# Last 512 tokens of the second shared experts as two groups of 256, two routed results summed per chunk, idle products in TensorE's first holes

## What is computed

```
x = x + layernorm(attention(layernorm(x)))        # 32 heads of 8, 8 key/value heads, rotary, causal
x = x + layernorm(ffn(layernorm(x)))

# ffn, per token xt:
scores = sigmoid(xt @ w_router.T)                 # 8 experts, top 2, weights normalised to sum 1
out  = sum over the 2 chosen experts of weight * (silu(xt @ wg.T) * (xt @ wu.T)) @ wd.T
out += sum over the 2 shared experts of (silu(xt @ sg.T) * (xt @ su.T)) @ sd.T      # inner width 640
```

## Time and profile before

| | us |
|---|---|
| three timed runs, median | 674.14 |
| timed runs, lowest and highest | 672.01, 674.25 |
| profiled execution | 669.11 |
| its span, first to last instruction | 667.4 |
| TensorE busy | 634.4 (95%) |
| VectorE busy | 531.4 (80%) |
| ScalarE busy | 417.1 (63%) |
| GpSimd busy | 327.6 (49%) |

### The profile page before, as it was taken

The page is one execution under the profiler, slowest core; times in us unless marked ns, Lnnn a source line. Parts: engine busy times, 40 slices in busy tenths (PEclk is TensorE's granted clock), DMA queues, the critical chain, the costliest instruction groups (busy, mean ns, idle before and its releaser), DMA issues.

```text
span 667.4 us, 15193 instructions
## 1 busy us (share of the span) xinstructions
PE 634.4 (95%) x5872; PEld 511.4 (77%) x5872; DVE 531.4 (80%) x1052; ACT 417.1 (63%) x782; POOL 327.6 (49%) x519
## 2 busy tenths in 40 slices
PE   8888899999999979999998999999999999999994
PEld 6634455555555547888888999999999999888883
DVE  5789999999988743479769888888988888468885
ACT  2526688888887875542247877877877787422230
POOL 3225657766666762100275464455454530178854
PEclk9958999999999999999999999999999999999998
DMA  3954543657350000000366786877776764032221
GB/s 90 174 125 66 116 82 66 124 104 155 90 107 13 18 11 17 16 1 1 119 225 222 264 273 224 262 242 267 229 256 240 253 224 145 20 92 91 84 64 47
DMA packets 79671, 87.10 MB, mean 131 GB/s; under 512 B 54352, under 2 KB 69072, under 8 KB 79600
## 3 DMA queue, kind: packets, MB, share of 16 engines
q0 software_dynamic: 11872, 54.53, 24.8%
q1 hardware_dynamic: 67456, 31.21, 20.2%
q10 hardware_dynamic: 272, 0.39, 0.2%
HBM read 63.83 MB, written 9.31 MB: 110 GB/s over the span
## 4 chain that ended last, share of the span: by engine, by line
PE 75%; DVE 10%; issue 4%; ACT 3%; SPq 2%; POOL 2%; DMA 1%; another core or an unknown queue 1%; POOLq 0%; DVEq 0%; ACTq 0%
PE PS L539 71%; DVE NM L1031 3%; DVE NM L1027 2%; PE PS L550 2%; PE PS L745 1%; ACT PF L886 1%; SPq L1540 1%; SPq L1546 1%; POOL PF L1449 1%; POOL RS L1392 1%; ACT WH L841 1%; DVE X L1296 1%; DVE RR L992 1%; DVE WL L1315 1%
## 5 line engine op out<-in xcount | busy, mean ns | idle before, releaser
L1236 DVE TENSOR_TENSOR HF<-SS,PS 128x256 f32<-128x256 f32 (+2 forms) x141 | 68.7, 487 | 72.3 <-ACT SS L932 34.3
L1315 DVE TENSOR_TENSOR WL<-RAW,WH 128x768 fp32r<-128x768 f32 x125 | 118.4, 958 | 7.7 <-ACT WH L841 7.3
L932 ACT ACTIVATE SS<-PS 128x256 f32<-128x256 f32 (+2 forms) x141 | 62.0, 439 | 87.6 <-PE PS L539 75.9
L1449 POOL TENSOR_SCALAR_AFFINE_SELECT PF<-PF 128x512 f32<-128x512 f32 x128 | 83.2, 673 | 58.4 <-ACT PF L886 58.4
L539 PE MATMUL PS<-WH,HH 128*128 128x256 f32 x355 | 103.2, 291 | 1.3 <-DVE ACC L1246 0.8
L841 ACT ACTIVATE HH<-HF 128x256 fp32r<-128x256 f32 (+1 forms) x120 | 58.0, 484 | 73.3 <-DVE HF L1236 63.0
L841 ACT ACTIVATE WH<-RAW 128x768 fp32r<-128x768 f32 x125 | 103.4, 841 | 0.0
L886 ACT ACTIVATE PF<-PS 128x1536 f32<-128x1536 f32 x64 | 92.8, 1450 | 16.8 <-PE PS L539 15.2
L539 PE MATMUL PS<-WL,HH 128*128 128x256 f32 x355 | 100.3, 282 | 0.0
L539 PE MATMUL PS<-WH,HL 128*128 128x256 f32 x355 | 100.2, 282 | 0.0
L539 PE MATMUL PS<-XGH,WH 128*128 128x256 f32 x320 | 90.4, 282 | 1.7 <-DVE WL L1315 1.0
(11 more groups left out here) (203 smaller groups left out, 1429.2 us busy)
## 6 DMA issues: line engine op xcount, KB each, us to landing
ys<-YO SPq DMA_DIRECT2D x16, 256.0 KB
RAW<-in_wsh SPq DMA_DIRECT2D x4, 768.0 KB, 4.9
XT<-in_xt SPq DMA_DIRECT2D x8, 256.0 KB, 3.7
X<-in_x SPq DMA_DIRECT2D x8, 256.0 KB, 3.7
xn<-YY SPq DMA_DIRECT2D x16, 128.0 KB, 1.7
out<-X SPq DMA_DIRECT2D x16, 128.0 KB
ys<-YO SPq DMA_DIRECT2D x7, 128.0 KB
RAW<-in_wsh SPq DMA_DIRECT2D x2, 384.0 KB, 5.3
```

The source lines that it names most:

```text
L932: eng.activation(ss, both(i, bank(b))[0], ACT.Silu).then_inc(free[b] if dense(i) else silu, 1)
L1236: eng.tensor_tensor(hf, ss, both(c, bank(b))[1], ALU.mult).then_inc(free[b], 1)
L1315: eng.tensor_tensor(WL[q % 2][:, c], RAW[raw_of(q)][:, c], WH[q % 2][:, c].bitcast(F32), ALU.subtract).then_inc(w_lo, 1)
L1449: eng.affine_select(out=o, in_=o, pattern=[[0, 4], [1, 128]], base=0, channel_multiplier=-1, compare_op=ALU.is_ge, fill=0.0).then_inc(zero ...
```

## The change

1. The last group of 512 tokens of the second shared experts (tiles 12 to 15) becomes two groups of 256 tokens. `HALF` is the first chunk of these (136), and there are 146 chunks in all. `up` makes products of 256 columns there, `down` two parts in place of four, the first of the two groups in bank 4, the second in bank 5. Tiles 12 and 13 are combined and finished within the chunks; only tiles 14 and 15 are left for `last`. From `HALF` on one tile a chunk goes to `o_stats` and `finish`, in place of two.
2. `mix` goes two tiles a chunk in chunks 125 to 129 (0 to 9), then one a chunk until `mix 15` in chunk 135. GpSimd's gathers move with it.
3. Idle products: 35 behind `f_qkv 3` (34 before), 13 behind `early 0` (14 before), and new ones: 5 behind `early 1`, 3 behind `early 2`, 2 behind `early 3`.
4. `FRONT0` is a quarter step earlier from `f_qkv` on; `FRONT1` has `f_third`, `f_fourth`, `q`, `k`, `k_twice` one or two quarter steps later. On SyncE the transposes of tiles 2 and 3 come as q 2, k 2, q 3, k 3 in place of k 2, q 2, k 3, (loads and `constants()`), q 3: the loads and constants go with `k 3` and so stand behind both transposes. `b_route` is a quarter step earlier and one leftover attention step moves from ahead of chunk 4 to ahead of chunk 3.

```diff
-CHUNKS += [(NK + 1, c % IC, 1) for c in range(DENSE)]
+HALF = len(CHUNKS) + DENSE - IC
+CHUNKS += [(NK + 1, c % IC, 1) for c in range(DENSE + IC)]
...
-WARM = {"mean": (0, 12), "f_qkv": (3, 34), "early": (0, 14), "late": (0, 6)}
+WARM = {("mean", 0): 12, ("f_qkv", 3): 35, ("early", 0): 13, ("late", 0): 6, ("early", 1): 5, ("early", 2): 3, ("early", 3): 2}
 JOIN = 64
-LAST4 = NT - 4
+FINAL = NT - 2
...
-FRONT0 = {"f_stats": -108, "f_dev": -111, "f_qkv": -87, "f_taken": -87, "f_rope": -83, "f_first": -81, "f_second": -80,
-          "f_third": -77, "q": -77, "k": -74, "k_first": -81, "k_third": -80, "f_fourth": -77, "k_twice": -73}
+FRONT0 = {"f_stats": -108, "f_dev": -111, "f_qkv": -88, "f_taken": -88, "f_rope": -84, "f_first": -82, "f_second": -81,
+          "f_third": -78, "q": -78, "k": -75, "k_first": -82, "k_third": -81, "f_fourth": -78, "k_twice": -74}
 FRONT1 = {"f_stats": -98, "f_dev": -95, "f_qkv": -77, "f_taken": -78, "f_rope": -78, "f_first": -78, "f_second": -71, "f_third":
-          -68, "q": -60, "k": -59, "k_first": -77, "k_third": -71, "f_fourth": -67, "k_twice": -66}
+          -67, "q": -58, "k": -57, "k_first": -77, "k_third": -71, "f_fourth": -65, "k_twice": -64}
...
-        "b_norm2": 66, "b_turn2": 70, "b_high": 69, "b_low": 68, "b_route": 75, "b_kept": 73}
+        "b_norm2": 66, "b_turn2": 70, "b_high": 69, "b_low": 68, "b_route": 74, "b_kept": 73}
...
-TAILS = (3, 2, 1, 2, 2, 3, 1, 1, 3, 3, 1, 2, 1, 3)
+TAILS = (3, 2, 1, 3, 1, 3, 1, 1, 3, 3, 1, 2, 1, 3)
...
-        if LAST + 4 <= c < LAST + 2 + NT:
-            m = c - LAST - 2
-            out.extend(("mix", i) for i in ((2 * m - 4, 2 * m - 3) if m < 4 else (m,)))
+        if LAST + 4 <= c < HALF:
+            m = c - LAST - 4
+            out.extend(("mix", i) for i in ((2 * m, 2 * m + 1) if m < NT - 11 else (m + NT - 11,)))
         if c < NC + 1:
             out.extend(("finish", i) for i in done)
-            done = stats[:2]
-            stats = stats[2:]
+            n = 1 if c >= HALF else 2
+            done = stats[:n]
+            stats = stats[n:]
             out.extend(("o_stats", i) for i in done)
         elif c == NC + 1:
-            for t in range(4):
-                out.append(("last", LAST4 + t))
-            out.extend(("finish", LAST4 + t) for t in range(4))
+            for t in range(2):
+                out.append(("last", FINAL + t))
+            out.extend(("finish", FINAL + t) for t in range(2))
...
                     for m in range(2):
-                        o = bank(take(("up", c, m)))
+                        o = both(c, bank(take(("up", c, m))))[m]
...
-                parts = n if narrow(c) else 4 if dense(c) else 2
+                parts = wide_of(c) // 128
                 for k in range(parts):
-                    b = 4 + k // 2 if dense(c) else 4 + q % 2
+                    b = 4 + (c - HALF) // IC if c >= HALF else 4 + k // 2 if dense(c) else 4 + q % 2
```

More of the change, by code:

```diff
@@ L85, in wide_of, with tiles_of, group_of @@
 def wide_of(c):
-    return 128 * CHUNKS[c][2] if narrow(c) else 256 if DENSE <= c < LAST else 512
+    return 128 * CHUNKS[c][2] if narrow(c) else 256 if DENSE <= c < LAST or c >= HALF else 512
+def tiles_of(c):
+    if c >= HALF:
+        return range(NT - 4 + 2 * ((c - HALF) // IC), NT - 2 + 2 * ((c - HALF) // IC))
+    return range(4 * ((c if c < DENSE else c - LAST) // IC), 4 * ((c if c < DENSE else c - LAST) // IC) + 4)
+def group_of(i):
+    return LAST + IC * (i // 4) if i < FINAL else HALF + IC
 def ends(c):
@@ L286, in banks @@
         elif s[0] == "down" and CHUNKS[s[1]][1] == 0:
-            for b in (4 + sequence(s[1]) % 2,) if DENSE <= s[1] < LAST else (4, 5):
+            for b in (4 + sequence(s[1]) % 2,) if DENSE <= s[1] < LAST else (4 + (s[1] - HALF) // IC,) if s[1] >= HALF else (4, 5):
                 count[b] += 1
@@ L647, in up @@
                 if dense(c):
-                    tg = (c if c < DENSE else c - LAST) // IC
-                    for t in range(4):
-                        read(e, ("b_turn2", 4 * tg + t))
+                    n = wide_of(c)
+                    t0 = 128 * tiles_of(c)[0]
+                    for t in tiles_of(c):
+                        read(e, ("b_turn2", t))
                     for m in range(2):
-                        o = bank(take(("up", c, m)))
+                        o = both(c, bank(take(("up", c, m))))[m]
                         k6 = 0
@@ L748, in idle @@
             def idle(s):
-                i, n = WARM[s[0]]
-                for _ in range(n if s[1] == i else 0):
+                for _ in range(WARM.get(s, 0)):
                     mm(bank(7, 256, 384), mean[:, :], mean[:, :], True)
@@ L1238, in combine @@
             def combine(c):
-                tg = (c if c < DENSE else c - LAST) // IC
                 e.wait_ge(dn, c + 1)
-                for q in (2, 3, 0, 1) if c == DENSE - 1 else range(4):
-                    i = 4 * tg + q
+                tiles = tiles_of(c)
+                for i in (*tiles[2:], *tiles[:2]) if c == DENSE - 1 else tiles:
+                    q = i % 4
                     b, k = use["down", c - IC + 1, 4 + q // 2]
@@ L1343, in _ @@
                     q = i % 4
-                    b, k = use["down", LAST + IC * (i // 4), 4 + q // 2]
+                    b, k = use["down", group_of(i), 4 + q // 2]
                     e.wait_ge(free[b], k)
@@ L1349, in _ @@
                 elif what == "last":
-                    t = i - LAST4
-                    b = use["down", NC - IC, 4 + t // 2][0]
-                    if t % 2 == 0:
-                        e.wait_ge(dn4, t // 2 + 1)
+                    t = i - FINAL
+                    b = use["down", NC - IC, 5][0]
+                    if t == 0:
+                        e.wait_ge(dn4, 1)
                         for u in range(2):
@@ L1496, in _ @@
                     deviation(i, o_ve, o_rs, i)
-                elif what == "finish" and i < NT - 2:
+                elif what == "finish" and i < FINAL:
                     e.wait_ge(o_n, i + 1)
@@ L1578, in _ @@
                 elif what == "finish":
-                    if i < NT - 2:
+                    if i < FINAL:
                         e.wait_ge(o_y, i + 1)
```

13 lines of the change are left out of this document (6 added, 7 removed).

## The result

The changed kernel takes 675.62 us as the median of its runs (672.28 to 680.23), the kernel before, timed beside it, 673.29 us: ratio 1.0037, 95% interval 1.0023 to 1.0052, so +2.3 us. The profiled execution of the changed kernel has a span of 673.2 us at a mean granted clock of 0.985 (before: 667.4 us).

The account below looks back on a forecast made before the run. TensorE was taken to set the pace in the second shared experts, with VectorE and GpSimd nearly full. Terms +0.27 -3.1 +0.2 +4.8 +0.6 -0.5 = +2.3 us on the 674.14 us median gave 676.4 us, range 670.5 to 680.5.

Parts of the forecast that it names:

- same within 0.5%: Whole kernel: a time between 670.8 and 677.5 us, not told from no change; chance 0.51.
- the stall: Second shared experts: `RS` behind more gathers in GpSimd's queue makes `down 129` and `down 133` late, +4.8 us (3.6 to 5.5).
- the halves: Chunks of 256 tokens: GpSimd's additions stretch VectorE's instructions, +0.6 us, between nothing and 2.5.
- Narrower products: `up` of the last group: ten chunks of 256-column products, 14.28 us, in place of five of 512, 14.01 us; +0.27 us.
- The end: Behind the last product: two tiles left, not four; last write 2.3 us sooner, output DMAs another 0.85; -3.1 us in sum.
- The gap between the last `up` and `down`: Between the last `up` and last `down`, less `down` work lies at each step: +0.2 us, between 0 and 0.8.
- the second stall: `down 133`, waiting through `RS 5` behind six more gather issues (ending at 633.5): adds 0.4 us to the first, 4.8 in all.
- The prediction is wrong if the gathers turn out faster than 1.25 us: GpSimd's gathers: a stated sign of failure, if each is faster than 1.25 us when not shared with VectorE's work.
- VectorE's own load goes into waits that it has anyway: Denser `mix`: five more tiles mixed early, 1.00 us each on VectorE, fill its existing waits and add nothing.
- rival C: Chunks of 256 tokens go at GpSimd's and VectorE's pace, 2.5 us in place of 0.6: +4.2 us, 678.3; chance 0.16.
- The front: Start of attention: `q 3` ahead of the constants takes the shorter time, maxima transfer starts sooner; -0.5 us (-1.1 to +0.5).
- Rival B: Start of attention: idle products keep TensorE at 2.4 GHz, shrinking its 5.75 us on the chain; +0.7 us, 674.8; chance 0.12.

Follow-up runs that it names:

- e2: The kernel before with only the denser `mix` (two tiles in each of the first five chunks, then one): 672.74 us, ratio 1.0093.
- e9: The changed kernel, `finish` of tiles 0 to 7 taking an earlier norm's scale without waiting for `RS` (these tiles scaled wrongly): ratio 1.0046.
- e11: The kernel before with the denser `mix`, and `finish` of tiles 0 to 7 without the wait for `RS` (scaled wrongly): ratio 1.0058.
- e6: The changed kernel with GpSimd issuing the gathers of tile i+1, instead of i+3, with `mix i`: ratio 1.0097.
- e8: The kernel before with the denser `mix` and the gathers of tile i+1 issued with `mix i`: ratio 1.0096.
- e1: The changed kernel with the old `mix` schedule (two tiles per chunk only in the first two chunks, then one): 667.28 against 667.07 us, ratio 1.0006.
- e3: The kernel before with only the new front (stage tables of tiles 0 to 3, SyncE's order, new idle product counts): ratio 0.9996.
- e4: The kernel before with only `b_route` one slot earlier and one leftover step moved from position 4 to 3 in TAILS: ratio 1.0007.
- e5: The changed kernel itself, timed a second time: ratio 1.0044.
- e7: The changed kernel with GpSimd issuing the gathers of tile i+2, instead of i+3, with `mix i`: ratio 1.0055.
- e12: The changed kernel with `finish` of tiles 0 to 7 two chunks later and one `mix` moved from the fifth chunk to the tenth: 667.42 against 667.04 us, 1.0009.
- e10: The changed kernel with `finish` of tiles 0 to 7 placed two chunks later, whole computation kept: 668.94 against 668.98 us, ratio 0.9988.

## Why the prediction was right

The forecast was +2.3 us and 676.4 us; measured are +2.3 us (1.5 to 3.5) and 675.6 us, and the outcome "same within 0.5%" had the largest chance. That the number is so close is partly luck: the stall came out 1.1 us above its term and the halves 0.6 us below theirs, and the 674.14 us that I added to came out at 673.29 in twenty runs. By its steps:

- **Narrower products (+0.27).** In the changed kernel the `up` of the last seven chunks start from 649.07 to 661.87 us, 2.13 us apart, where I counted 2.14. Ten of them are 21.3 us, five of 4.24 are 21.2. The term is +0.1.
- **The end (-3.1).** To the last write 4.29 us in place of 6.45, -2.2 for the -2.3 forecast; behind it 3.08 in place of 3.60, so -0.5 for -0.85. In all -2.7, and the same to 0.01 us in every kernel with the split.
- **The gap between the last `up` and `down` (+0.2).** The last product ahead of the last chunk's `down` starts at 663.88 and the next at 664.45, 0.57 us apart. Before, the same two were 0.38 us apart (654.13 and 654.51): +0.2.
- **The stall (+4.8).** The delay from GpSimd's queue was right in place and size. `RS 3` ends at 619.38, which is 617.07 on the old axis, as `HF 121` starts 2.31 us later; forecast 617.25. `down 129` is 4.3 us late, forecast 4.4. In e2, where nothing else is changed, the second stall at `down 133` brings it to 4.8 us, as forecast. In the changed kernel the sum is larger, 5.9 us, for something that I hadn't in it, the half clock behind the hole. The granted clock is 0.50 from 623 to 625 us, and the delay of TensorE's starts against those of before (each axis from its own `HF 121`) grows from 4.35 us at `down 129` to 5.87 us by the end of the next `up`, 1.5 us more. With this the second stall vanished: `RS 5` ends at 635.11 us, 632.80 on the old axis where 633.5 was forecast, but TensorE was by then later than that. Two smaller holes ahead, at `down 127` and `down 128`, don't add to it, as GpSimd's queue is the chain of waits all along. The first comes with `HF` and `SS` late for TensorE's semaphores (last section), the second is in e2 as well, without these.
- **What the stall is made of.** Here the reasoning fell short. I put it down to the wait of `finish` for `RS` alone. e9 and e11 show that without this wait 3.7 to 4.2 us of it stay in their traces (in e9 1.4 of these by the clock), by the wait of `mix` for the gathered rows, and e6 to e8 that issuing later only exchanges the one for the other. The cause is GpSimd's queue: e2 makes the stall with the denser `mix` alone, the changed kernel's chain of waits stays on GpSimd from the first gather to `RS 3`, and VectorE stands idle for its results (`RS` or gathered rows) at the stall of each run that has one. At two tiles a chunk its issues need 5.0 us in a chunk of 4.24, and whatever of its work VectorE needs next is late. "The prediction is wrong if the gathers turn out faster than 1.25 us" named the right quantity and too narrow a consequence.
- **"VectorE's own load goes into waits that it has anyway".** The load did. But I had treated the denser `mix` as a cost without a return, and e1 shows the return: 2.8 us that e1 loses from `down 134` on are avoided by it. Without it the change would be at +0.4 us, not at the -2.5 that my terms give. This is the largest error in the sum's structure, and it doesn't show in the sum because the change has both parts.
- **The halves (+0.6), rival C.** After the stall the delay grows from 5.87 to 6.20 us, and the two terms above, 0.1 and 0.2, are all of it: the halves cost nothing, C (+4.2) did not happen. e1 loses 2.8 us there, but not by C's single additions: behind 642 us, where a chunk has at most one, it has no hole ahead of the last `down`.
- **The front (-0.5).** `HF 0` starts at 254.97 to 255.90 in eight of nine profiles with the new front and at 255.81 to 257.49 in the five without it, medians 255.2 and 256.1, so about -0.9 us (both kinds spread by some 2 us); timed by itself -0.3 us (-1.1 to +0.6). Consistent with -0.5, not measured better. The working behind it failed: `q 3`, which ahead of the loads was to take 2.04 us, takes 3.03 there in e3 (from 33.27 us), against 3.24 behind them in e4. Whether the transfer lands later by the loads right ahead of it isn't seen: it takes 2.16 and 2.17 us.
- **Rival B.** The clock held at 1.00 over 34 to 42 us, but B's price did not come: the 5.75 us on the chain, which were to shrink, are 5.69 in e3 and 5.89 in the changed kernel, since from 44 to 48 us the granted clock is 0.50 in both. The objection to B, that TensorE goes on waiting behind 34 us where no idle product stands, was the right one. e3 gains 0.3 us in all.

With the measured sizes: 0.1 - 2.7 + 0.2 + 5.9 = +3.5 us for the last phase, less 0.3 to 0.9 for the front, is +2.6 to +3.2, inside the measured 1.5 to 3.5.

## What to carry to other kernels

When a change lets one engine's work come denser, compare the denser rate with the rate of the engine that feeds it, before asking which single wait comes last: here 5.0 us of GpSimd's issues in a 4.24 us chunk, and each wait that was removed uncovered the next one from the same queue. Look also at what a part that seems to be only a cost makes room for elsewhere, and undo it by itself before calling it a loss. Split the span at a marker that all variants share: the stretch from `HF 121` to the last product came out the same to 0.01 us in the three kernels in which it should (before, e3, e4), while their spans differ by 2.5 us.

## What the runs showed of the hardware

**A hole can cost a second time in clock.** Behind a long hole of TensorE in this phase the granted clock fell to 0.50 in six profiles, and it stayed at 1.00 in three. The holes are measured from start to start of the two products, and the cost is what the starts behind the hole lose against 0.2335 and 0.119 us apart:

| kernel | hole, us | stretch with clock 0.50, us | cost, us |
|---|---|---|---|
| e6 | 4.2 | 616.6 to 622 | 2.6 |
| e8 | 4.1 | 619 to 622 | 1.6 |
| e5 | 3.35 | 623 to 625 | 1.5 |
| changed | 3.1 | 623 to 625 | 1.5 |
| e9 | 3.1 | 616 to 619 | 1.4 |
| e7 | 2.2 | 643 to 646 | 1.5 |
| e2 | 3.55 | none | 0 |
| e11 | 3.05 | none | 0 |
| e12 | 2.35 | none | 0 |

The length of the hole alone doesn't decide: e7's is shorter than all three that cost nothing. What does isn't settled by these runs.

**TensorE's results seen late.** At the first routed chunks ScalarE's `SS` waits for a product that the trace shows as done long before. The changed kernel, last product of chunk 20's `up`, and `SS` of it:

```profile
343.26 0.29 PE L552 MATMUL PS<-XGH,WL 128*128 128x256 f32 x1
```

```profile
347.59 0.38 ACT L945 ACTIVATE SS<-PS 128x256 f32<-128x256 f32 x1 [4.97 <-remote]
```

"remote" says that the profile finds nobody who ended the wait. The semaphore that `SS` waits for changed 4.0 us after the product's recorded end. The same two waits of `SS` are in the profile of e8, whose code up to there is that of the kernel before, and not in that of e3 (waits of ScalarE in 342 to 352 us, e8 first):

```profile
ACT SS L932 <- remote: 5.2, 2, 4.9
```

```profile
ACT SS L931 <- PE PS L539: 3.4, 3, 1.4
```

So it isn't the change's. Such waits are there in all nine profiles of three series (the first pair, e5 to e8, e9 to e11) and in none of the five of e1 to e4 and e12, and these are the series in which the kernel before had its median at 673.3, 673.2 and 669.0 us, against 667.1 and 667.0. In eight of the nine it happens again between 604 and 611 us (not in the kernel before). Most of the difference between the series in the stretch from `HF 0` to `HF 121` arises at this place: between `HF 0` and `HF 33` the kernel before, e9, e10 and e11 lose 1.7 to 1.8 us against e4, the changed kernel and e5 to e8 4.4 to 6.1 us, and e1, e2, e3 and e12 nothing. Whether the semaphores are late or the recorded times of the products early can't be told from a trace; the engines that wait do start late. A difference between two profiles at such a place must not be put down to the code.
